# Attention with a mixture-of-experts layer: the query projections moved under the maximum, the residual added by TensorE

## The reference

```python
# x (16, 256, 128), ctx (16, 64, 128)
q, k, v = norm(x) @ Wq.T, ctx @ Wk.T, ctx @ Wv.T           # 16 heads of 8
attn = softmax(q @ k.T / sqrt(8), axis=1)                   # axis 1 is the head axis: over the 16 heads
x = x + (attn @ v) @ Wo.T
h = norm(x)
x = x + h + shared experts(h) + routed experts(h)           # 2 shared, 2 of 8 routed, erf gelu, F = 512
```

## Time and profile before

| | |
|---|---|
| median of three runs | 428.0 us (426.48 to 429.03) |
| the profiled execution | 428.38 us, of which the span of the trace is 426.6 us |
| TensorE busy | 322.9 us (76%) |
| VectorE busy | 311.8 us (73%) |
| ScalarE busy | 282.2 us (66%) |
| GpSimd busy | 270.3 us (63%) |
| first and last maximum (L875) | 27.5 and 141.2 us |

### The profile page before, as it was taken

One profiled execution on the slowest core, in us unless ns is written; L12 is line 12 of the kernel. 1 busy time (PEld: TensorE's weight loads), 2 busy tenths in 40 slices (PEclk: granted clock), 3 DMA queues, 4 the chain that ended last, 5 costly groups with the idle time before them and its releaser, 6 DMA issues.

```text
span 426.6 us, 12009 instructions
## 1 busy us (share of the span) xinstructions
PE 322.9 (76%) x4112; PEld 249.0 (58%) x4113; DVE 311.8 (73%) x628; ACT 282.2 (66%) x530; POOL 270.3 (63%) x274
## 2 busy tenths in 40 slices
PE   5776866666676677879987898789999999999300
PEld 1464443434443454556655576569898998999300
DVE  4789577898899958994869765647676676676257
ACT  3878576778587655458956688546667675767165
POOL 6436646789888790377677783507777777777600
PEclk9999699978998956889989999989999999999855
DMA  8963222231000000011111440131332322321097
GB/s 262 310 206 143 74 75 85 91 89 38 2 2 2 2 2 0 14 51 51 39 51 52 124 88 14 46 93 51 102 83 82 86 77 74 90 83 55 10 343 248
DMA packets 28892, 36.17 MB, mean 85 GB/s; under 512 B 4900, under 2 KB 23975, under 8 KB 28336
## 3 DMA queue, kind: packets, MB, share of 16 engines
q1 hardware_dynamic: 24304, 27.13, 20.8%
q0 software_dynamic: 4544, 8.44, 6.2%
HBM read 21.74 MB, written 14.72 MB: 85 GB/s over the span
## 4 chain that ended last, share of the span: by engine, by line
PE 38%; DVE 22%; issue 16%; POOL 13%; DMA 5%; ACT 4%; SPq 1%; POOLq 1%; DVEq 0%; ACTq 0%
DVE Z L880 5%; POOL results L505 5%; POOL E L425 4%; PE banks L1516 3%; PE banks L1515 3%; PE banks L1501 3%; PE banks L1502 3%; PE banks L1503 3%; PE banks L1433 3%; PE banks L1517 3%; DVE E L954 2%; PE banks L1435 2%; PE banks L1437 2%; DVE Mx L875 2%; PE banks L1417 2%
## 5 line engine op out<-in xcount | busy, mean ns | idle before, releaser
L505 POOL DMA_INDIRECT results<-E,qRep x78 | 86.5, 1109 | 43.9 <-issue 27.3
L495 POOL DMA_INDIRECT gathered<-xs,slot x64 | 66.7, 1042 | 43.9 <-issue 18.6
L425 POOL TENSOR_TENSOR E<-E,rZ 128x1024 f32<-128x1024 f32 x32 | 68.3, 2158 | 22.8 <-DVE rZ L883 22.8
L1171 DVE TENSOR_TENSOR E<-hid,E 128x512 f16<-128x512 f32 x78 | 54.0, 692 | 37.8 <-ACT E L747 36.7
L745 ACT ACTIVATE hid<-banks 128x512 f32<-128x512 f32 x78 | 46.9, 601 | 43.7 <-PE banks L1503 25.2
L954 DVE TENSOR_TENSOR E<-hid,E 128x512 f16<-128x512 f32 x64 | 45.8, 730 | 17.3 <-ACT E L708 16.7
L707 ACT ACTIVATE hid<-banks 128x512 f32<-128x512 f32 x64 | 38.7, 605 | 29.8 <-PE banks L1419 28.1
L1433 PE MATMUL banks<-wprojL,E 128*128 128x128 f16 x256 | 48.2, 225 | 13.5 <-DVE E L954 13.4
L1515 PE MATMUL banks<-wprojL,E 128*128 x312 | 56.4, 219 | 1.8 <-DVE E L1171 0.9
L1517 PE MATMUL banks<-wprojH,E 128*128 x312 | 55.8, 219 | 0.0
L1516 PE MATMUL banks<-wprojH,E 128*128 x312 | 55.8, 219 | 0.0
(11 more groups left out here) (206 smaller groups left out, 831.2 us busy)
## 6 DMA issues: line engine op xcount, KB each, us to landing
qRep<-gathered SPq DMA_DIRECT2D x39, 129.0 KB, 2.2
qRep<-q_rows SPq DMA_DIRECT2D x32, 128.0 KB, 2.5
qRep<-results SPq DMA_DIRECT2D x8, 512.0 KB, 6.8
X<-in_x SPq DMA_DIRECT2D x4, 512.0 KB, 6.1
q_rows<-qRep SPq DMA_DIRECT2D x8, 256.0 KB, 2.1
out<-X SPq DMA_DIRECT2D x8, 256.0 KB, 3.4
xs<-in_wproj_t SPq DMA_DIRECT2D x1, 1536.0 KB, 6.6
results<-E,qRep POOLq DMA_INDIRECT x78, 2.7
```

Of the source, the lines that this page charges most:

```text
L425: g.tensor_tensor(heads, heads, rZ[:, k % 2, :].unsqueeze(1).unsqueeze(3).broadcast_to([P, HH // 2, P, 2]), ALU.mult).then_inc(attn_ready, 1)
L495: g.indirect_dma_start(out=gathered, out_offset=bass.IndirectOffsetOnAxis(ap=slot[:, k, i:i + 1], axis=0), in_=xs[:, i, :], in_offset=None ...
L505: g.indirect_dma_start(out=results, out_offset=bass.IndirectOffsetOnAxis(ap=xg[:, k, h, 2 * D:ROW].bitcast(I32), axis=0), in_=yg[:, k, h, ...
```

## The change

There are four edits, and GpSimd's and SP's lists are as they were.

1. `prologue_rest` stands straight behind `raw_scores` on TensorE. `high_q` stands ahead of the exponentials on ScalarE. `low_q(u + 1)` is taken in unit u, where `low_q(u)` was.
2. `project_out` of units 0 to 4 moves behind `minus_max`; from unit 8 on it keeps its place.
3. From the sixth unit on (`FROM = 5`) TensorE adds the residual, with one more product of the unit matrix and `X` into `y_ps`. ScalarE copies the sum to `X` (`copy_x1`), and VectorE's addition is gone from the units that follow.
4. `ffn_transposes` stands behind `raw_scores` too, ahead of `project_out` and `minus_max`. ScalarE's `copy_x2` comes ahead of its `add_norm`. At the end of the attention `copy_o(UNITS - 1)` stands ahead of `sigmoid_exps(0)`.

```diff
+            def copy_x1(u):
+                act.wait_ge(y_ready, u + 1)
+                s.activation(X[:, u // 2, :, u % 2, :], y_ps[:, 0:2 * D].rearrange("p (b d) -> p b d", b=2), ACT.Copy
+                             ).then_inc(x_added, 1)
...
+                    if 0 < u < PAIRS - 1:
+                        high_q(u + 1)
                     exps(u, k, not first)
                     if not (first and k < 2):
-                        if not first:
+                        if u - 3 >= FROM:
+                            copy_x1(u - 3)
+                        elif not first:
                             act.wait_ge(y_ready, u - 3)
                         copy_o(u - 2, k)
...
                     if k in (1, 2) and not (first or second):
-                        add_norm(n - 2, k - 1)
                         if third and k == 1:
                             act.wait_ge(low_ready[4], 4)
                         copy_x2(2 * n - 5 + k)
+                        add_norm(n - 2, k - 1)
...
-            act.wait_ge(y_ready, UNITS - 3)
+            copy_x1(UNITS - 3)
             copy_o(UNITS - 2, 0)
             for pair in (LATE, LATE + 1):
                 copy_x2(pair)
+            copy_x1(UNITS - 2)
+            copy_o(UNITS - 1, 1)
             sigmoid_exps(0)
-            act.wait_ge(y_ready, UNITS - 2)
-            copy_o(UNITS - 1, 1)
+            copy_x1(UNITS - 1)
...
-                    if second or first and k > 1:
-                        low_q(u)
-                    if not (first and k < 3):
-
+                    if first and k or second and k < 3:
+                        low_q(u + 1)
+                    if second or first and k == 3:
                         add_attention(u - 3, (k + 1) % 2, 2 * n + (k - 3) // 2)
...
-            add_attention(UNITS - 1, 1, PAIRS - 1)
             place(0, 0)
...
+                if u >= FROM:
+                    last = t.matmul(y_ps[:, 0:2 * D].rearrange("p (b d) -> p b d", b=2), ident[:],
+                                    X[:, u // 2, :, u % 2, :], start=False, stop=True, skip_group_check=True)
                 last.then_inc(y_ready, 1)
...
                     raw_scores(u, k, 2 * n + k // 2, first and k == 0)
-                    if first and k < 3:
-                        keep_going(6)
-                    if first and k == 3:
-                        pe.wait_ge(wo_loaded, 16 * 4 * NGRP)
-                    if not (first and k < 3):
-                        project_out(u - 3, (k - 3) % 4, first and k == 3)
+                    if u < PAIRS:
+                        prologue_rest(u)
+                    if first and k == 0:
+                        keep_going(4)
+                    if n == 2 and k == 1:
+                        pe.wait_ge(qlo_ready, PAIRS)
+                    if k in (1, 2) and inputs:
+                        ffn_transposes(2 * n - 5 + k, n > 2 or k > 1)
+                    if u >= PAIRS:
+                        project_out(u - 3, (k - 3) % 4, False)
...
                     minus_max(u, k)
+                    if first and k == 3:
+                        pe.wait_ge(wo_loaded, 16 * 4 * NGRP)
+                    if 3 <= u < PAIRS:
+                        project_out(u - 3, (k - 3) % 4, u == 3)
                     if values:
                         for half in range(2):
                             weighted_values(u - 2, (k - 2) % 4, half)
-                    if u < 2 * 4:
-                        prologue_rest(u)
-                    if n == 2 and k == 1:
-                        pe.wait_ge(qlo_ready, PAIRS)
-                    if k in (1, 2) and inputs:
-                        ffn_transposes(2 * n - 5 + k, n > 2 or k > 1)
```

More of the change, by code:

```diff
@@ L58 @@
 LATE = PAIRS // 2
+FROM = 5
 PORTIONS = ((0, TILES - 2 * TP), (TILES - 2 * TP, TILES))
@@ L607, in prologue_rest @@
             def prologue_rest(u):
-                if 0 < u < PAIRS - 1:
-                    high_q(u + 1)
                 if u < PAIRS - 2:
@@ L931, in late_low @@
                                 ).then_inc(late_ready, 1)
-            add_attention(UNITS - 3, 1, PAIRS - 2)
             for j in range(2):
@@ L936, in _ @@
                 late_low(LATE + j, j)
-            add_attention(UNITS - 2, 0, PAIRS - 1)
             def add_shared(pair, j):
@@ L1325, in project_out @@
                         last = t.matmul(y_ps[:, D * b:D * b + D], oT[:, k % 2, half], wo[:, b, half],
-                                        start=(half == 0), stop=(half == 1))
+                                        start=(half == 0 and (b == 0 or u < FROM)), stop=(half == 1 and u < FROM),
+                                        skip_group_check=(u >= FROM))
+                if u >= FROM:
+                    last = t.matmul(y_ps[:, 0:2 * D].rearrange("p (b d) -> p b d", b=2), ident[:],
+                                    X[:, u // 2, :, u % 2, :], start=False, stop=True, skip_group_check=True)
                 last.then_inc(y_ready, 1)
```

## The result

The changed kernel takes 431.84 us (median of 20 runs, 428.33 to 435.17) against 427.98 us (20 runs, 426.17 to 429.90). The medians differ by 3.9 us. The ratio is 1.0076, with a 95% interval from 1.0053 to 1.0099, which is 0.76% or 3.3 us slower; it leaves out the three longest executions of the changed kernel, the profiled one (435.17 us) among them, as slow ones. The profiled span is 433.4 us against 426.6. Its trace alone could show what only the longest executions have, so the main readings stand beside those of e6_two_late_units_back, a kernel that differs in two units and whose profiled execution took 430.73 us.

A forecast was written before the change was run, and what follows sets the result against it. Early units bound by a VectorE-TensorE loop, around unit 9 by GpSimd; -7.5 + 9.7 + 1.1 + 3.0 = +6.3 us, held at +6, giving 434.0 us, range 431.5 to 436.5.

The forecast's parts named there:

- Term A: Early units 2 to 7: projections and query transposes run under VectorE's maximum; -7.5 us, between -8.3 and -3.7.
- the ring: Units 2 to 7: a loop through VectorE and TensorE sets the pace, 43.64 us for five units before the change.
- Term B: Units 9, 10, 13, 14: moved transposes wait for GpSimd's low half or ScalarE's copy_x2, delaying the next maximum; +9.7 us.
- Term D: Units 9 and 13: TensorE's clock falls to half after the long waits, slowing the work behind; +3.0 to +4.4 us.
- Term C: End of the attention: product ahead of the router, sigmoid's exponentials later, VectorE's last addition gone; +1.1 us.
- The faster one: Rival, units 9 and 13: low halves are ready when the scores are written, so no wait; 421.6 us, chance 0.11.
- ScalarE did not bound the early units: Denies the rival that ScalarE bounds the early units, gain there only -3.7 us; 437.8 us, chance 0.10.
- the queries' move does nothing: Rival, early units: projections still wait for ScalarE's high half and only losses are left; chance next to nothing.
- The case in which the clock stays up: Rival, units 9 and 13: clock does not fall or is back at once; 431.3 us, chance 0.19.

The follow-up runs named there:

- e6_two_late_units_back: Changed kernel with ffn_transposes put back behind the values in units 10 and 14 alone; 430.93 us against 428.28 for the kernel before.
- e1_transposes_back: Changed kernel with ffn_transposes of units 9, 10, 13 and 14 back behind the values; 506.62 us against 511.88 for the kernel before.
- e2_only_transposes: Kernel before with only ffn_transposes moved ahead of the subtraction and copy_x2 ahead of add_norm; 521.14 us against 511.88.
- e5_filler: Changed kernel with filler products on TensorE ahead of the transposes of units 9 and 13, x2_ready wait moved ahead; 430.02 us against 428.28 for the kernel before.
- e11_end_as_before: Kernel of e1_transposes_back with the sigmoid's exponentials ahead of the last copy_o again; 504.40 us against 511.93 for the kernel before.
- e7_two_early_units_back: Changed kernel with ffn_transposes put back behind the values in units 9 and 13 alone; 433.04 us against 428.28 for the kernel before.
- e8_transposes_later: Kernel before with the queries' move and project_out's, plus ffn_transposes and copy_x2 one unit later, transposes behind the subtraction; 419.10 us against 428.28.

## Why the prediction held

**Term A** (-7.5 us). S - T(0) is 8.5 us shorter. T(2) to T(7) was put at 34.7 us and is 34.36, T(2) - T(0) at 0.6 us more and is 0.5 more (13.23 against 12.70). The 0.8 us that I took off for ScalarE's list were not needed. Their reason, that lists so even cannot both be full, does not hold here: from 53.8 to 65.9 us neither ScalarE nor VectorE has a wait in the trace. What the prediction did not see is that 1.7 of the 43.64 us were half clock in unit 2 and not the ring; without them the gain is 6.8 us.

**Terms B and D** (+9.7 and +3.0 to +4.4). From S to T(15) were 53.18 us and are 65.10, +11.9. Piece by piece: T(10) at S + 23.6, or S + 25.8 with the clock's 2.2, is S + 25.28. T(11) - T(10), put at 8.4, is 7.98. T(14) - T(13), put at 10.0 and 1.5 to 2.2 more with the clock, is 11.71; the low half came at T(13) + 4.8 and not 0.4 earlier as I had it. T(15) - T(14), put at 8.4, is 7.96. The subtraction of unit 13, for which I had announced a granted clock of 0.5, was at full clock again. The waits of about 7 and 4.5 us are 7.07 and 4.91. In e1_transposes_back and e2_only_transposes the mechanism is shown from both sides. The two terms can be told apart by e5_filler, where the clock stayed up behind both long waits: T(10) is S + 23.14 and T(14) - T(13) 9.60 us there, 0.5 and 0.4 less than B had. From the start of the transposes to the next maximum it has 5.16 us in both units, where the changed kernel has 7.23 and 6.88, so the clock costs 2.1 and 1.7 us, and D is 3.8. The Trainium skill's rule of waits that let the clock fall ("TensorE: Matmul & The Clock Gate", section "HAM oscillation — how this bites in real kernels") is borne out by e5_filler: with the wait filled, `project_out` behind it fell from 2.02 to 1.11 us. The length of a wait does not decide alone, since there 1.64 us were followed by half clock too, and 1.73 and 1.74 us in the changed kernel were not.

**Term C** (+1.1). Slots - T(15) is 1.3 us more. The order of the last copy is worth 1.0 us in e11_end_as_before, where the whole end is 1.95 us longer; in the changed kernel's own trace the exponentials start 0.9 us after their input is ready.

**The size.** Forecast was +6 us, measured +3.9, or 3.3 by the ratio; 431.84 us lies near the lower end of the forecast's own range of 431.5 to 436.5. In the trace the terms are -8.5, +11.9 and +1.3, together +4.7 where the sum had +6.3. Term A was mis-sized by 1.0 us, of which 0.8 are the deduction for ScalarE. Term B, 9.7 us, is 7.9 by the distances without the clock's part (3.8 in unit 9, 2.6 in unit 13, and 0.75 and 0.73 in units 10 and 14, which were put at 1.2 each). Term D was counted at its lower end, 3.0, and is 3.8. That the profiled execution, 435.17 us against 428.38, is 6.8 us longer and so close to the sum of +6.3 is luck: 0.7 of it is a later start of the first maximum, 4.7 are the terms, and 1.4 arise behind the slots, for which the prediction had nothing.

The half clock in units 9 and 13 is not peculiar to the longest executions. In e6_two_late_units_back, 430.73 us, T(10) is at S + 25.28 and T(14) - T(13) is 11.68, as in the changed kernel's trace. What differs is the stretch from the slots to the end of the span, with TensorE's mean granted clock in its first 120 us:

| | slots to the end | granted clock |
|---|---|---|
| before | 250.6 | 0.95 |
| changed | 252.0 | 0.93 |
| e5_filler | 252.9 | 0.93 |
| e7_two_early_units_back | 252.2 | 0.93 |
| e6_two_late_units_back | 249.2 | 0.96 |
| e8_transposes_later | 249.8 | 0.96 |

The code behind the slots is the same in all six. So these executions differ by up to 3.7 us there, as much as the measured change, and the differences go with the clock. Over the twenty runs of the changed kernel the time and the mean granted clock go together as well: the five shortest (428.33 to 429.49 us) have clocks of 0.914 to 0.919, the five longest (434.55 to 435.17) have 0.895 to 0.907. Those runs have no trace, so where in them the clock fell is not shown, nor is it shown whether the change makes the fall among the experts more frequent.

**The rivals.** The faster one needed the low half by T + 2.3; it ended at T(9) + 6.8. ScalarE did not bound the early units: T(2) to T(7) came out at 34.36 us, VectorE's list. That the queries' move does nothing is refuted by the same number. The case in which the clock stays up, 431.3 us, is nearest to the median in its number, and its picture is still wrong: the rows of units 9 and 13 show half clock behind both long waits. That the time came close to it is the work of mis-sized terms, and in part luck.

## What to carry to other kernels

A step that is moved under another engine's work must have its inputs by then. The projections had, and the early units became 8.5 us shorter. The transposes moved with them waited 7 and 5 us for GpSimd ahead of the subtraction, for which ScalarE's exponentials and through them VectorE and the next scores wait, and took that back. Put a wait for a slow producer behind the instruction that releases the others, not ahead of it. The queries' move with the transposes behind the subtraction and one unit later is 2.2% faster than the kernel before (interval 1.8 to 2.6); by the traces the queries' move carries that gain, and a gain from the transposes' later place is not shown. When several such waits follow one another, taking one away gains little, since the next one takes its place.

## What was not expected of the hardware

- TensorE's clock stayed at full through 6.07 us of filler and 1.58 us idle, but the clock fell one unit later after only 1.64 us of idle time, where in the changed kernel 1.74 us at 138.98 had no such effect.
- One and the same program takes 428 us on one chip and 512 us on two others, at equal durations of the instructions and of the early units. ScalarE and VectorE have waits among the experts there, of up to 15.1 and 30.4 us at a time, that the other chip's traces do not have. Whether these make up the 84 us, and what they wait for, is open.
- The runs of the changed kernel spread over 6.8 us (428.33 to 435.17) where those of the kernel before spread over 3.7 beside it. On the chip of e5 to e8 the kernel before spreads over 6.0 itself (424.97 to 431.00, without its longest), so the spread is not the change's own.
- ScalarE and VectorE can both be full: for 12 us of the early units, from 53.8 to 65.9 us, neither waits for the other.
